# Output matmuls of two small-head attentions: values stationary in four column groups, denominators spread by a matmul, reciprocal as exp(-ln)

## The reference

```
# causal: squared softplus in place of the exponential
p = softplus(q @ k.T * 8**-0.5) ** 2 * tril
attn = p / (sum(p, -1) + 1e-9)
x = layernorm(x + (attn @ v) @ w_proj.T + b_proj)
# cross: q and k rotated by position, keys masked in the first cross attention
attn = softmax(q @ k.T * 8**-0.5)
x = layernorm(x + (attn @ v) @ Wout)
```

## Time and profile before

| | |
|---|---|
| time, median of 3 runs (lowest, highest) | 781.32 us (778.82, 783.33) |
| span of the profiled execution | 788.8 us |
| TensorE busy | 633.0 us, 80% |
| VectorE busy | 505.0 us, 64% |
| ScalarE busy | 381.3 us, 48% |
| GpSimd busy | 230.7 us, 29% |
| mean granted TensorE clock | 0.869 |

### The profile page before, as it was taken

The page is one execution under the profiler, slowest core; times in us unless marked ns, Lnnn a source line. Parts: engine busy times, 40 slices in busy tenths (PEclk is TensorE's granted clock), DMA queues, the critical chain, the costliest instruction groups (busy, mean ns, idle before and its releaser), DMA issues. The chain is left out here.

```text
span 788.8 us, 12952 instructions
## 1 busy us (share of the span) xinstructions
PE 633.0 (80%) x3779; PEld 513.6 (65%) x3786; DVE 505.0 (64%) x1221; ACT 381.3 (48%) x966; POOL 230.7 (29%) x254
## 2 busy tenths in 40 slices
PE   4898885999999968699889999979999988781006
PEld 3777774777777756467668888868777776430006
DVE  3788983656675745744544444447677676469886
ACT  3778883445444532133235444435455463484615
POOL 3555552323222211356500000014334331005220
PEclk9899996989997958899979999989899797695558
DMA  5400000001000000000000000001010000000001
GB/s 158 160 11 10 10 13 14 21 21 28 24 20 17 0 1 1 0 1 2 1 11 7 11 10 7 17 14 27 20 26 21 19 17 0 1 0 0 0 0 54
DMA packets 30649, 15.29 MB, mean 19 GB/s; under 512 B 18513, under 2 KB 29841, under 8 KB 30610
## 3 DMA queue, kind: packets, MB, share of 16 engines
q1 hardware_dynamic: 30610, 14.82, 6.7%
HBM read 10.09 MB, written 1.05 MB: 14 GB/s over the span
## 5 line engine op out<-in xcount | busy, mean ns | idle before, releaser
L330 PE MATMUL bank<-a_mov,a_stat 128*128 128x256 f32 x256 | 84.2, 459 | 12.0 <-issue 10.2
L514 DVE TENSOR_REDUCE rowmax<-bank 128x8 f32<-128x512 f32 x64 | 44.2, 691 | 62.2 <-PE bank L330 61.4
L330 PEld LDWEIGHTS bank<-a_mov,a_stat 128*128 128x128 f32 x256 | 50.6, 219 | 28.7 <-issue 23.0
L1213 POOL TENSOR_TENSOR e_hid<-e_gated,e_relu 128x512 f32<-128x512 f32 x32 | 40.6, 1270 | 57.0 <-DVE e_gated L1328 56.8
L1088 PEld LDWEIGHTS bank<-body_sb,e_hid 128*128 128x128 f32 x288 | 37.7, 196 | 22.0 <-issue 13.9
L139 POOL TENSOR_TENSOR xb<-X,made_bias 128x128 f32<-128x128 f32 x32 | 14.6, 457 | 117.2 <-DVE r L149 103.8
L1190 ACT ACTIVATE e_relu<-bank 128x512 f32<-128x512 f32 x36 | 21.5, 598 | 54.2 <-PE bank L1066 45.1
L1328 DVE TENSOR_TENSOR e_gated<-e_relu,bank 128x512 f32<-128x512 f32 x32 | 21.9, 686 | 36.6 <-PE bank L1076 22.5
L252 POOL TENSOR_TENSOR a_stat<-qk,head_sb 128x512 f32<-128x512 f32 x32 | 33.3, 1041 | 37.5 <-ACT qk L405 36.3
L330 PE MATMUL bank<-l_mov,l_stat 128*128 128x256 f32 x128 | 42.3, 462 | 2.2 <-POOL l_mov L252 2.0
L469 ACT ACTIVATE oT<-bank 64x64 f32<-64x64 f32 x192 | 41.7, 217 | 4.1 <-PE bank L375 2.0
(11 more groups left out here) (262 smaller groups left out, 1716.3 us busy)
## 6 DMA issues: line engine op xcount, KB each, us to landing
kvT<-in_ctxT SPq DMA_DIRECT2D x64, 64.0 KB, 2.1
xs<-X SPq DMA_DIRECT2D x56, 64.0 KB, 1.9
body_sb<-in_body SPq DMA_DIRECT2D x2, 950.0 KB, 5.1
body_sb<-in_body SPq DMA_DIRECT2D x2, 949.5 KB, 5.2
out<-X SPq DMA_DIRECT2D x4, 256.0 KB, 2.3
X<-in_x SPq DMA_DIRECT2D x1, 896.0 KB, 6.0
mid_sb<-in_mid SPq DMA_DIRECT2D x1, 448.0 KB, 3.6
head_sb<-in_head SPq DMA_DIRECT2D x1, 422.0 KB, 3.2
```

What stands on the lines that cost most here:

```text
L330: mm = nc.tensor.matmul(psS[b][:, 256 * half:256 * half + 256], m.stat[:, par, b, 2 * half:2 * half + 2, :], m.mov[:, par, b, :, :], start ...
L514: nc.vector.tensor_reduce(m.rowmax[:, b, :], psS[b][:, :].rearrange("p (x k) -> p x k", k=T), AX.X, ALU.max).then_inc(s[f"max_done{b}"].se ...
L1213: nc.gpsimd.tensor_tensor(m.hid[:, n % DEEP, :], a, m.relu[:, n % DEEP, :], ALU.mult).then_inc(s["hid_ready"], 1)
```

## The change

The same products are computed with the operands' roles exchanged. For each sequence, each pair of head parities c and each group i of four heads, 32 columns of values (three quarters of them zero) are stationary, and 64 columns of probabilities move. The output of group i goes to the partitions 32i to 32i + 31, so the four values of i use four column groups of TensorE. The channels come out on the partitions, as `project_outputs` wants them: the transpose, the four copies and `small_out` go. The denominators must stand beside every channel, so a second set of 16 matmuls with a constant 0/1 matrix (`own_head`) as the stationary operand spreads them over the same partitions, into columns of the bank that also holds the result of `project_outputs`. ScalarE makes their reciprocal as exp(-ln(d)), two activations of 128 x 128, and VectorE multiplies once. The orders of all three engines are rewritten; in the cross attentions the steps from `project_outputs` to `apply` move one slot later.

```diff
-        def outputs(t, par, b):
+        def outputs(t, par):
             wait(pe, s["o_ready"], t)
+            wait(pe, s["r_done"], t)
             wait(pe, s["v_ready"], t + 1)
-            wait(pe, s[f"prob_ready{b}" if causal else f"pT_ready{b}"], t + 1)
-            for i in range(NI):
-                lhsT = m.prob[:, par, b, i, :, :] if causal else m.probT[:, b, i, :]
-                at = 36 * (NI * b + i)
-                mm = nc.tensor.matmul(psO[:, at:at + 36], lhsT, m.vals[:, par, b, i, :, :, :], start=True, stop=True)
-            mm.then_inc(s[f"o_psum{b}"].sem, 1)
-        def turn_outputs(t, par):
-            wait(pe, s["r_done"], t)
-            wait(pe, s["o_ready"], t + 1)
-            nc.tensor.transpose(psOY[:, 0:P], m.o[:, par, :, :], m.ident).then_inc(s["oT_psum"].sem, 1)
+            for b in range(SB):
+                wait(pe, s[f"prob_ready{b}" if causal else f"pT_ready{b}"], t + 1)
+            for of_values in (False, True):
+                for b in range(SB):
+                    for c in range(2):
+                        for i in range(NI):
+                            rhs = m.prob[:, par, b, i, c, :] if causal else m.probT[:, b, i, c * T:(c + 1) * T]
+                            lhsT = m.vals[:, par, b, i, 32 * c:32 * c + 32] if of_values else m.own_head[:, c, :]
+                            ps = psO if of_values else psD
+                            mm = nc.tensor.matmul(ps[32 * i:32 * i + 32, b * T:(b + 1) * T], lhsT, rhs, start=(c == 0), stop=(c == 1))
+                mm.then_inc(s["o_psum" if of_values else "d_psum"].sem, 1)
...
# TensorE
             if causal:
-                run(turn, 0), run(scores1, 1), run(project_outputs, 3), run(project, 0), run(outputs0, 2)
-                run(outputs1, 2), run(values, 0), run(scores0, 0), run(turn_outputs, 2)
+                run(turn, 0), run(scores1, 1), run(project_outputs, 3), run(project, 0), run(outputs, 2)
+                run(values, 0), run(scores0, 0)
             else:
-                run(turn, 0), run(scores0, 1), run(outputs1, 2), run(project, 0), run(scores1, 1), run(turn_probs0, 1)
-                run(values, 0), run(turn_outputs, 2), run(outputs0, 1), run(project_outputs, 2), run(turn_probs1, 1)
+                run(turn, 0), run(scores0, 1), run(project_outputs, 3), run(project, 0), run(outputs, 2)
+                run(scores1, 1), run(turn_probs0, 1), run(values, 0), run(turn_probs1, 1)
...
# ScalarE
-        def copy_outputs(t, par):
-            wait(act, s["oT_psum"], t + 1)
-            wait(act, s["y_psum"], t)
-            for b in range(SB):
-                for c in range(2):
-                    op = nc.scalar.activation(m.oT[c * T:(c + 1) * T, 0, b * T:(b + 1) * T],
-                                              psOY[b * T:(b + 1) * T, c * T:(c + 1) * T], ACT.Copy)
+        def log_denominators(t, par):
+            wait(act, s["d_psum"], t + 1)
+            if causal:
+                nc.scalar.activation(m.lnden[:, :], psD, ACT.Ln, bias=m.tiny[:, 0:1]).then_inc(s["lnden_done"].sem, 1)
+            else:
+                nc.scalar.activation(m.lnden[:, :], psD, ACT.Ln).then_inc(s["lnden_done"].sem, 1)
+        def reciprocals(t, par):
+            wait(act, s["lnden_done"], t + 1)
+            wait(act, s["o_ready"], t)
+            nc.scalar.activation(m.rden[:, :], m.lnden[:, :], ACT.Exp, scale=-1.0).then_inc(s["rden_done"].sem, 1)
...
             if causal:
-                run(copy_turned, 0), run(copy_qk, 0), run(exponential0, 1), run(log_one_plus0, 1), run(exponential1, 1)
+                run(copy_turned, 0), run(copy_qk, 0), run(exponential0, 1), run(log_one_plus0, 1)
+                run(log_denominators, 2), run(reciprocals, 2), run(exponential1, 1)
                 run(log_variance, 3), run(log_one_plus1, 1), run(copy_values, 0), run(rstd, 3), run(square0, 1)
-                run(copy_outputs, 2)
             else:
                 run(rstd, 4), run(exponential1, 2), run(copy_values, 1), run(copy_probs1, 2), run(copy_turned, 0)
-                run(exponential0, 1), run(copy_probs0, 1), run(log_variance, 3), run(copy_outputs, 2)
+                run(exponential0, 1), run(copy_probs0, 1), run(log_denominators, 2), run(reciprocals, 2), run(log_variance, 3)
...
# VectorE
+            wait(dve, s["o_psum"], t + 1)
             wait(dve, s["rden_done"], t + 1)
+            wait(dve, s["y_psum"], t - 1)
+            nc.vector.tensor_tensor(m.oT[:, par, :], psO[:, 0:P], m.rden[:, :], ALU.mult).then_inc(s["o_ready"].sem, 1)
...
             if causal:
                 run(softplus1, 1), run(apply, 3), run(scale_and_mask0, 0), run(clamp0, 0), run(residual, 2)
                 run(scale_and_mask1, 0), run(statistics, 2), run(variance, 2), run(clamp1, 0)
-                run(denominators, 1), run(reciprocals, 1), run(normalise, 1), run(softplus0, 0)
+                run(normalise, 1), run(softplus0, 0)
             else:
-                run(maximum0, 1), run(less_maximum0, 1), run(reciprocals, 2), run(rotate, 0), run(normalise, 2)
-                run(variance, 3), run(maximum1, 1), run(less_maximum1, 1), run(apply, 3), run(residual, 2)
-                run(statistics, 2)
+                run(apply, 4), run(maximum0, 1), run(less_maximum0, 1), run(residual, 3), run(statistics, 3), run(rotate, 0)
+                run(variance, 3), run(maximum1, 1), run(less_maximum1, 1), run(normalise, 2)
```

88 lines of the change are left out of this document (29 added, 59 removed).

## The result

The changed kernel takes 793.98 us (median of 4 runs, 791.04 to 797.15); the kernel before, run beside it, takes 782.33 us (4 runs, 778.82 to 789.48). The ratio is 1.0161, with a 95% interval of 1.0103 to 1.0219: slower by 1.6%, or 12 us, where the forecast was 22 us and its range began at 785. Some executions of either kernel take about a per cent longer at a lower granted clock; the ratios leave these out, the medians do not. The profiled executions are 5.5 us apart in their spans, 794.3 against 788.8; the one of the kernel before was among its slower ones, 1% above its median, so sums over the two profiles understate the change.

The account below looks back on a forecast made before the run. The prediction took a serial loop, set by where scores1 stands in TensorE's order, to bound the cross slots, and ScalarE the causal. Causal -4.5, masked +19.5, biased +12, drains -4: about +22 us on 781.3, 803 us; range 785 to 832.

Parts of the forecast that it names:

- The ring of the cross stages: Serial slot loop: outputs waits for the previous tile's residual, delaying scores1; masked slot 8.47 to 9.75 us, biased 7.94 to 8.7.
- The outputs pass: TensorE, each tile: 64 narrow passes in four overlapping column groups, 0.9 us plus two switches, 1.1 instead of 1.87 us.
- Rival 4: Outputs matmuls: the column groups don't overlap, +2.7 us on 45 slots, about 920 us; chance 0.05.
- The wait inside ScalarE: Cross slots: copy, Ln, Exp, lnvar and rstd all precede exponential1, which starts at +8.4 us in the masked slot.
- The causal step: Causal slot: ScalarE closes the loop, losing 0.93 and gaining 0.6 to 0.7 us; -0.3 a slot, -4.5 us.
- The clock: Cross stages: more TensorE idling puts 22 to 25% of time at 1.2 GHz, costing 0.28 us per us there.
- Drains: Last tiles of each cross stage lose copies, transpose and a VectorE pair, about 2 us each; -4 us.
- Rival 1: Cross slots: TensorE's streaming bounds them and the residual wait is not felt; -30 us, 751 us; chance 0.10.
- Rival 2: Denser column-grouped passes keep the clock at 2.4 GHz throughout; +2 us, 783 us; chance 0.08.
- Rival 3: Cross stages: longer idle stretches lower the clock for near half the time; +49 us, 830 us; chance 0.12.
- the signs that the prediction named: Outputs 1.0 to 1.2 us, just after the residual; TensorE idle about a microsecond before; slots 9.5-10, 8.5-9, 6.3-6.4 us.
- masked term: Masked cross stage: +1.3 us a slot over 15 full slots, +19.5 us.

Follow-up runs that it names:

- e1_bank: Changed kernel with the spread denominators moved to the free half of the outputs' bank, so project_outputs, not outputs, waits for the residual; 781.35 us, ratio 0.9966 to before.
- e4_late: Changed kernel with TensorE issuing scores1 before outputs in the cross stages; 785.17 us, ratio 0.9985 to the kernel before.
- e2_twice: Changed kernel with the 16 denominator matmuls of each tile issued twice, same result; 811.39 us, ratio 1.0354 to the kernel before.
- e6_serial: Changed kernel with the outputs matmuls issued column group by column group instead of alternating; 826.83 us, ratio 1.0549 to the kernel before.
- e7_recip: Changed kernel with VectorE's reciprocal in place of ScalarE's Ln and Exp in the cross stages; 772.56 us, ratio 0.9845 to the kernel before.
- e3_turn: Changed kernel with turn writing its own bank in the causal stage, so values waits for copy_values instead; 789.84 us, ratio 1.0135 to the kernel before.
- e8_apply: e3_turn with VectorE running scale_and_mask0 ahead of apply in the causal stage; 782.3 us, ratio 1.0014 to the kernel before.
- e5_fill: e1_bank plus five unread constant matmuls behind values in each cross slot, where TensorE idled; 750.38 us, ratio 0.9553 to the kernel before.
- e11_before_fill: Kernel before the change plus two unread constant matmuls behind project_outputs in each cross slot; 764.35 us, ratio 0.977 to the unfilled kernel before.
- e9_all: Changed kernel with the edits of e1_bank, e3_turn, e8_apply and e7_recip together; 752.5 us, ratio 0.9637 to the kernel before.
- e12_after_fill: Changed kernel plus five unread constant matmuls at the head of values in each cross slot; 781.23 us, ratio 0.9938 to the kernel before.
- e10_all_fill: e9_all plus the five unread constant matmuls behind values in each cross slot; 740.29 us, ratio 0.9463 to the kernel before.

## Why the prediction was right, and where its sizes were off

**The ring of the cross stages** came out as written. From the turn of the masked slot, forecast and measured: maximum0 +1.90 and +1.91, end of less_maximum0 +3.41 and +3.41, outputs +3.9 and +3.71, scores1 +5.3 and +5.06, the probability copy +6.9 and +6.66, the second exponential +8.4 and +8.10, the next turn +9.75 and +9.32. Most of the 0.43 us too much is the way from the end of less_maximum0 through the residual to outputs (0.47 assumed, 0.30 measured, the residual's start overlapping the subtraction's end) and the last step from turn_probs1 to the turn (0.59 assumed, 0.46 measured). That the wait for the residual is the cause is shown by e1_bank and e4_late, each of which takes 0.6 to 0.95 us a slot back at full clock; e2_twice shows that the passes are on the ring. The remark that even with outputs at no cost the slots would be 8.65 and 7.6 holds against 8.47 for the masked slot; for the biased one 7.6 lies below the old 7.94. Biased: 8.7 forecast, 8.25 in the early slots; but over 13 slots at a held clock 111.4 / 13 = 8.57 against 103.6 / 13 = 7.97 before, so +0.60 for the forecast +0.8. Masked in the same way 9.12 against 8.42, +0.71 for the forecast +1.3: this term of the sum was mis-sized most, 19.5 us where 15 x 0.71 = 11 would have been right.

**The outputs pass** was priced at 0.9 us for both parts and 0.1 for each switch. The trace has 0.45 and 0.45 between starts, and 1.04 us from the first start to the mask row. The rule of the Trainium skill (TensorEngine Tiling (Array Packing), section Instruction Overhead) that was weighed against it, 60 cycles for each matmul, would have given 1.6; the trace does not agree with it, since 32 passes in 0.45 us are 14 ns or 34 cycles each. Issued group by group, as in e6_serial, they take 36 ns or 86 cycles each, so the order decides. Rival 4 is refuted by e6_serial, which shows what a lost overlap costs.

**The wait inside ScalarE** (Ln and Exp in front of exponential1) stood in the prediction's chain as a leg and not as a finding. e7_recip shows its worth: 0.42 us of lateness in each slot, as much as half of the wait for the residual.

**The causal step failed.** "ScalarE closes the loop, and it loses 0.93 and gains 0.6 to 0.7: -0.3" gave -4.5 us. The slot at full clock went from 6.64 to 6.82, so the term is +2.7 at full clock. I read a nearly full ScalarE in the earlier trace rows as the loop, and a mean of 76 us in 89 as VectorE's slack. In a full-clock slot of the kernel before VectorE was busy for 6.08 of 6.64 us: its whole list was the ring, and the four copies came in only through the 0.19 us that the residual waited. The change took about 0.9 us out of that list, but the slot did not get it. The ring now runs through VectorE (softplus1, apply, scale_and_mask0, clamp0, residual, scale_and_mask1, clamp1) and back through ScalarE's second exponential and logarithm; `apply` came to stand beside GpSimd's square (0.34 to 1.10 us), and `turn` to wait for copy_values. e3_turn shows that the wait of `turn` costs the 0.18 us, and e8_apply that with `apply` out of the way the slot falls by another 0.6 to 0.67, to 5.97 to 6.05, well below the old one.

**The clock.** I took 22 to 25% of the time at 1.2 GHz for the cross stages; the mean clocks 0.89 and 0.93 mean 22 and 14%, and the causal stage went the other way, from 0.91 to 0.99, which is what hid its longer slots (87.5 us for 89.1). The reason that I gave, idle time of one to two microseconds, is half supported: e5_fill takes the low clock away by filling it and e7_recip by shortening it from 1.78 to 1.38 us, but the kernel before has no idle time over 0.6 us in the slots of the earlier trace rows, was no better off, and e11_before_fill cures it with 0.45 us of work. What lets the clock fall in that kernel stays open. That e9_all lost it again fits the idle time: before turn_probs1 of its biased slots TensorE idles 1.92 to 2.10 us in every second one, more than in the changed kernel (clock 0.92), in its masked slots mostly 1.38 (0.97). The price that I gave a microsecond at 1.2 GHz in the new ring, 0.28 us, was nearly right; measured is about 0.2, against 0.4 in the old one.

**Drains** were put at -4 us; outside the three windows the changed kernel gained 4.7 in the profiled run, 2.6 of it where the causal stage hands over to the masked one. Between e11_before_fill and e12_after_fill what lies outside is 0.9 us longer instead, with two slots of each stage in it. No run measures the drains alone.

Rival 1 (751 us) is refuted by the idle 0.82 us and by e1_bank. Rival 2 (783) needed a held clock, which did not come; with it, e12_after_fill is 5 us below the unfilled old kernel (0.9938), where this rival had it 2 us above, and still stands 1.7% above its filled counterpart. Rival 3 (830, a sum without the causal term of -4.5) did not come. Of the signs that the prediction named, the gap, the start 0.1 us after the residual and the times of Ln and Exp are there; the full-clock slots are outside the forecast in the masked stage (9.2 to 9.3 for 9.5 to 10) and the causal one (6.8 for 6.3 to 6.4), and in the biased one partly so (8.25 to 8.84 for 8.5 to 9).

The forecast of 803 against 794 is thus the right mechanism in the cross stages, with a masked term 8 us too high and a biased one 3 us too high, and the wrong one in the causal stage, 7 us too low. Corrected in this way its 22 us are 18. The spans of e12_after_fill and e11_before_fill lie 18.3 apart, their ratios 13; with the drains not shown, the close match with the first is partly chance. The measured 12 us are within the error of both. Part of what is missing from 18 can be the clock, which took 5 us more from the old cross windows than from the new ones, in single executions. And the total owes something to luck: with the causal term right and the others as they were, it would have been 29.

## What to carry to other kernels

A step that is moved in a list carries its waits past everything that stands behind it: here some 0.8 us of saved TensorE work a slot (110 us busy to 99 over 13 masked slots) was paid for with a wait for VectorE that a different bank, or one swap in the list, takes away (e1_bank, e4_late), and a reciprocal that was put on the idle-looking ScalarE stood in front of the one activation on which the slot hangs (e7_recip). A full engine is not the ring: follow one slot from a step to the same step of the next tile before pricing what leaves the fullest engine. And compare two kernels at the same granted clock before explaining a per cent or two, by filling their idle time if need be: the 5.4% of e10_all_fill are 3.1% against the old kernel with filling of its own (0.9463 / 0.977 = 0.969). In the windows 9.1 us of that gain lie in the causal stage, 4.7 in the masked and 1.5 in the biased one: the saved work shows most where VectorE's list had been the ring, though the clocks there still differ (0.98 against 0.94).

## What the runs showed of the hardware

- Matmuls of 64 moving and 32 stationary columns in four column groups, fp32: 32 instructions in 0.45 us when the groups alternate, in 1.15 us when they follow each other group by group.
- A VectorE tensor_scalar from SBUF to SBUF beside a GpSimd instruction that began first: 1.10 us for 0.34, and 1.00 to 1.23 for 0.43 (clamp1 against clamp0); scalar_tensor_tensor from PSUM beside the same instruction keeps its 0.68.
- VectorE's reciprocal of 128 x 128 takes 0.92 us, three times the multiply's 0.29; ScalarE's Ln and Exp of that size take 0.27 (0.35 with a bias tile) and 0.31.
- A microsecond at 1.2 GHz in the cross stages cost about 0.4 us in the kernel before (15.8 us for some 37) and 0.2 in the changed one (10.6 for some 44).
- Two matmuls on constants in each slot of 8 us lifted the mean granted clock of the two cross stages of the kernel before, in which TensorE was already 91 to 94% busy, from 0.93 and 0.91 to 1.00, and took 2.3% off the whole kernel's time.
